# One block for three attention layers: a node queue across layers, three weight batches in the last, two rings of six

## The reference

```python
src_f = concatenate([src, loop]); dst_f = concatenate([dst, loop])      # every node has an edge to itself
def layer(h_in, p):
    h = h_in @ Wl
    a = (h @ asl)[src_f] + (h @ adl)[dst_f] + ea_f @ (Wel @ ael)
    a = where(a > 0, a, 0.2 * a)
    m = segment_max(a, dst_f); ea = exp(a - m[dst_f]); denom = segment_sum(ea, dst_f)
    out = segment_sum(h[src_f] * (ea / denom[dst_f])[:, None], dst_f) + bl
    return layernorm(out) * gl + bel
h, _ = scan(layer, x, (W, att_src, att_dst, W_e, att_edge, bias, ln_gamma, ln_beta))
x = layernorm(x + h)
```

## Time and profile before

| | |
|---|---|
| three timed runs | 4970.62, 4992.32, 4992.92 us (median 4992.32) |
| span of the profiled execution | 4946.1 us |
| time of the profiled execution as a whole | not recorded apart from its span |
| PE busy, mean granted clock | 3008.1 us (61%), 0.744 |
| DVE busy | 2621.4 us (53%) |
| ACT busy | 2248.3 us (45%) |
| POOL busy | 1924.2 us (39%) |
| HBM | 152 GB/s over the span |

### The profile page before, as it was taken

One profiled execution on the slowest core, in us unless ns is written; L12 is line 12 of the kernel. 1 busy time (PEld: TensorE's weight loads), 2 busy tenths in 40 slices (PEclk: granted clock), 3 DMA queues, 4 the chain that ended last, 5 costly groups with the idle time before them and its releaser, 6 DMA issues. The chain is left out here.

```text
span 4946.1 us, 67111 instructions
## 1 busy us (share of the span) xinstructions
PE 3008.1 (61%) x18033; PEld 2422.5 (49%) x18033; DVE 2621.4 (53%) x8048; ACT 2248.3 (45%) x5931; POOL 1924.2 (39%) x1994
## 2 busy tenths in 40 slices
PE   1183019997887786885663059981089930387864
PEld 1062007775443454443662049970089930377764
DVE  2083008998443665895662017760047730399875
ACT  0082008886111344674552027760057730387765
POOL 6605760000554554563665720007600047200366
PEclk7596559998777788997776569875589865698555
DMA  3293016664554343454663237652257642376542
GB/s 116 69 334 112 12 38 213 223 223 174 147 156 122 94 115 111 134 171 136 193 199 114 63 112 226 201 171 63 61 178 219 206 133 59 112 242 224 160 129 88
DMA packets 419336, 723.48 MB, mean 146 GB/s; under 512 B 76431, under 2 KB 137908, under 8 KB 418606
## 3 DMA queue, kind: packets, MB, share of 16 engines
q1 hardware_dynamic: 350990, 610.53, 37.7%
q0 software_dynamic: 63040, 107.35, 8.8%
q10 hardware_dynamic: 5024, 2.30, 0.2%
HBM read 428.65 MB, written 321.10 MB: 152 GB/s over the span
## 5 line engine op out<-in xcount | busy, mean ns | idle before, releaser
L663 POOL DMA_INDIRECT msgs<-t_gat,row_i x591 | 564.5, 955 | 1097.5 <-POOLq L161 913.7
L2193 ACT ACTIVATE t_nnt<-t_p_nt,cxt 128x512 f32<-128x512 f32 x294 | 200.5, 682 | 767.1 <-remote 250.6
L1718 PE MATMUL t_p_q<-mean_col,t_nsq 128*128 128x1 f32 x2352 | 336.7, 264 | 265.0 <-issue 242.3
L1718 PEld LDWEIGHTS t_p_q<-mean_col,t_nsq 128*128 128x128 f32 x2352 | 347.8, 227 | 273.0 <-issue 272.9
L679 POOL DMA_INDIRECT dg_g_ring<-t_xw,src_i x197 | 190.2, 965 | 653.9 <-DVE slot_id L1182 580.2
L2073 PE MATMUL t_p_nt<-ident,t_nh 128*128 128x128 f32 x1176 | 220.5, 320 | 306.8 <-issue 175.5
L1987 POOL DMA_INDIRECT out_rows<-t_x,own_i x197 | 201.4, 1022 | 487.1 <-ACT t_x L2243 433.0
L1711 PE MATMUL t_p_nh<-wx,t_nnt 128*128 128x132 f32 x1568 | 268.1, 323 | 175.3 <-issue 132.0
L2073 PEld LDWEIGHTS t_p_nt<-ident,t_nh 128*128 128x128 f32 x1176 | 161.0, 165 | 325.5 <-issue 229.9
L1711 PEld LDWEIGHTS t_p_nh<-wx,t_nnt 128*128 128x128 f32 x1568 | 231.3, 224 | 176.4 <-issue 175.8
L1732 DVE TENSOR_TENSOR t_nhn<-t_p_nh,t_ninv 128x264 f32<-128x264 f32 x392 | 151.4, 428 | 260.0 <-remote 143.2
(11 more groups left out here) (402 smaller groups left out, 8599.3 us busy)
## 6 DMA issues: line engine op xcount, KB each, us to landing
t_nh<-t_gat SPq DMA_DIRECT2D x294, 264.0 KB
t_gat<-t_nhn SPq DMA_DIRECT2D x196, 264.0 KB
t_x<-de_x SPq DMA_DIRECT2D x196, 256.0 KB
t_ah<-t_gat SPq DMA_DIRECT2D x150, 264.0 KB
t_x<-t_x SPq DMA_DIRECT2D x148, 256.0 KB
t_gat<-t_ahn SPq DMA_DIRECT2D x100, 264.0 KB
t_gat<-de_h SPq DMA_DIRECT2D x98, 264.0 KB
t_xw<-in_x_map SPq DMA_DIRECT2D x28, 903.0 KB
```

Source lines behind the costliest of these rows:

```text
L663: self.nc.gpsimd.indirect_dma_start(out=self.msgs[:, c, 0:width], out_offset=None, in_=table, in_offset=bass.IndirectOffsetOnAxis(ap=idx[: ...
L1718: last = self.nc.tensor.matmul(p_q[:, j:j + 1], sq[:, j * D:(j + 1) * D], self.mean_col[:], start=True, stop=True)
L2193: nc.scalar.activation(nnt[:, g % 2], p_nt[:], ACT.Identity, bias=bias).then_inc(act_nt, 1)
```

## The change

The three calls become one, `phase_gats`, with one block and one plan of 342 ticks for all three layers.

- The 294 node groups stand in one queue. It doesn't stop at the end of a layer: ticks 102 to 113 take the first groups of layer 1 beside the last slot groups of layer 0, and ticks 198 to 227 the first 30 of layer 2 beside the end of layer 1. The node part of a table depends on no slot, so only the gathers wait for the slot groups of the layer before: POOL waits for their stores (`rows_stored`) in place of the barrier.
- Layer 2 has three weight batches. Its pieces stand in ticks 257 to 264, 277 to 285 and 298 to 306. Slot groups 0 to 4 enter in ticks 265 to 269, the others from 292 on (`HELD` keeps them back), and the queue of nodes ends at tick 299. Of the ticks from 300 on 42 hold slot work alone.
- The ring `x` of ten is split: `xn` with six buffers for nodes, and `held`, six laid over the buffers of `nhn` and `ahn`, for slots. The rings `nh` and `ah` shrink from four buffers to three, `tt` from three to two.
- In the last stage the constant is added first (`slot_beta`, `node_beta`), and DVE scales one of a slot group's four tiles (`slot_scale`), where ACT scaled all four.

```diff
-XR = 10
+NR = 3
+XR = 6
-LAST_BATCHES = ((0, ROWP),)
-PLAN = BATCHES, (96, 190, 290), 2.6, 2.6
-LAST_PLAN = LAST_BATCHES, (280,), 3.4, 5.0
+READY = 96, 190, 290
+NODE_TIME = 2.6, 2.6, 3.4
+SUM_TIME = 2.6, 2.6, 5.0
+HELD = 240
...
+    for layer in range(L):
+        last = layer == L - 1
...
+            elif not own and pieces and at - begun >= READY[pieces[0][1]]:
+                w = pieces.pop(0)
+            held = last and a >= XR - 1 and at - begun < HELD
+            i = None
+            if a < end and (a < open_to or open_to == AG) and not held:
+                i, a = (layer, a), a + 1
+            m = None
+            if n < NODES + 6:
+                m, n = n, n + 1
+            plan.append((m, i, w))
...
             def _(pool):
-                for b, (r0, r1) in enumerate(batches):
-                    self.resident_gather(self.row_i, self.th[layer], XW, got[b], range(2 * r0, 2 * r1))
+                for layer in range(L):
+                    if layer > 0:
+                        rows_stored(pool, nout, layer * DG)
+                        rows_stored(pool, aout, layer * AG)
+                    for b, (r0, r1) in enumerate(BATCHES):
+                        self.resident_gather(self.row_i, self.th[layer], XW, got[b], range(2 * r0, 2 * r1))
...
+                for g in range(AG):
+                    pool.wait_ge(xa_act, g + 1)
+                    pool.wait_ge(xa_dve, g + 1)
...
+                        if g >= XR:
+                            sp.wait_ge(xput[g % XR], 16 * G4 * (g // XR))
+                        sp.dma_start(held[:, g % XR], self.slots(self.x3, 0, g)).then_inc(xarra[g % XR], 16)
...
+                def slot_result(k):
+                    act.wait_ge(xa_inv, k + 1)
+                    for j in range(G4 - 1):
+                        r = nc.scalar.activation(held[:, k % XR, j, :], held[:, k % XR, j, :], ACT.Copy, scale=iva[:, k % 3, j:j + 1])
+                    r.then_inc(xa_act, 1)
...
 def resnorm_gnn(nc, args, out):
-        for layer in range(3):
-            net.phase_gat(layer)
+        net.phase_gats()
```

More of the change, by code:

```diff
@@ L45 @@
 EVERY = 5
-XR = 10
+NR = 3
+XR = 6
+L = 3
+NODES = L * DG
 BATCHES = ((0, 32), (32, 64), (64, ROWP))
-LAST_BATCHES = ((0, ROWP),)
-PLAN = BATCHES, (96, 190, 290), 2.6, 2.6
-LAST_PLAN = LAST_BATCHES, (280,), 3.4, 5.0
[L53 to L71, removed]
+READY = 96, 190, 290
@@ L1930, in phase_gat @@
[L1930 to L1938, removed]
+            got = [sem(f"got{b}") for b in range(len(BATCHES))]
@@ L1957, in phase_gat @@
[L1957 to L1972, removed]
+                if a is not None and 0 <= a[1] - 3 < AG:
+                    roots["a", a[0] * AG + a[1] - 3] = len(roots) + 1
+            batch_of = lambda g: [b for b, (r0, r1) in enumerate(BATCHES) if 2 * r0 <= g * G4 < 2 * r1][0]
@@ L2046, in _ @@
+                for n, a, w in plan:
                     if n is not None:
@@ L2220, in sums @@
-                    if 0 <= i - 4 < AG and not last_layer:
-                        g = i - 4
-                        act.wait_ge(dve_ahn, g + 1)
-                        nc.scalar.activation(self.att_s[:, g * G4:(g + 1) * G4, :], ahn[:, g % 3, :, D:D + 3], ACT.Copy).then_inc(act_att, 1)
-                def weights(b, part):
-                    rows = slice(*batches[b])
+                        s = layer * AG + i - 2
+                        act.wait_ge(dve_as, s + 1)
+                        wait(act, pe_ah, s - 1)
@@ new lines, in slot_beta, with slot_row @@
+                def slot_beta(k):
+                    dve.wait_ge(xarra[k % XR], 16 * (k // XR + 1))
+                    nc.vector.tensor_tensor(held[:, k % XR], held[:, k % XR], self.each(self.bet[:]), ALU.add).then_inc(xa_bet, 1)
+                def slot_row(k, s):
+                    dve.wait_ge(xa_bet, k + 1)
+                    for j in range(G4):
+                        y = nc.vector.scalar_tensor_tensor(out=held[:, k % XR, j, :], in0=p_ah[:, k % 2, j * D:(j + 1) * D],
+                                                           scalar=ainv[:, s % 2, j:j + 1], in1=held[:, k % XR, j, :],
+                                                           op0=ALU.mult, op1=ALU.add)
+                    y.then_inc(xa_y, 1)
```

582 lines of the change are left out of this document (327 added, 255 removed).

## The result

The changed kernel took 4993.63 us (median of 20 runs, 4965.91 to 5014.46), the kernel before on the same chip 4967.69 us (20 runs, 4936.09 to 5010.7). The ratio is 1.0048, with a 95% interval of 1.003 to 1.0065: slower by half a per cent, at the edge of what I had called no change. The forecast was 5001 us, with +9 us for the change itself; the medians give +26. That 5001 lies only 7 us above 4993.63 is in part luck: the median that I started from, 4992.32, is 25 us above that of the 20 runs, and the change cost 17 us more than forecast.

What follows compares the result with a forecast made beforehand. PE bounds node groups in layers 0 and 1 and pairs, DVE slot groups and layer 2's node groups; gathers nearly dead, no engine full in the scatter. Terms sum to +9 us, giving 5001 us, range 4930 to 5070.

Steps and rivals of the forecast that it cites:

- step 6: Between the layers: two block ends go, -4 us (low -8, high 0).
- step 7: Last stage: DVE scales one tile of each slot group, 50 times, +6 us (0 to +12).
- step 8: Buffer rings: smaller rings, six held buffers and first slot loads no longer issued ahead, +2 us (0 to +40).
- step 4: Layer 2: two more weight batches, priced from the one of before, +38 us (+14 to +60).
- step 1: End of layer 0: 12 ticks of slot work become pairs with node groups, +15 us.
- step 2: End of layer 1, ticks 206 to 227: 22 mixed ticks of 6.7 us, +64 us (+60 to +113).
- step 3: Thirty node groups leave layer 2, -98 us; eight replace cheaper groups in layer 1, +9; together -89 us.
- step 5: Gathers of layers 1 and 2: more node groups use the 20 us before the stall, -23 us (-23 to 0).
- rival A: Scatter: constant, sum and scale no longer queue behind PE's late result; -48 us, to a total of 4953 us; chance 0.27.
- B: Ticks 206 to 227: PE's clock falls to 1.2 GHz, ticks take 8.9 us; +48 us, total 5055 us; chance 0.15.
- C: Scatter: SP waits for the ring of six, DVE behind it; +42 us, total 5043 us; chance 0.16 together with D.
- D: Layer ends: the stalled gathers keep the node queue from running ahead; +42 us; chance 0.16 together with C.

Runs made afterwards that it cites:

- second chip: Chip with the stall, where both kernels and variants of the change were run; kernel before 4934.5 us, changed kernel 4946.75 us, ratio 1.0031.
- first pair: First profiles of the kernel before and the unaltered changed kernel, compared layer by layer; the kernels' medians there were 4967.69 and 4993.63 us.
- third chip: Chip without the stall, where the unaltered change and variants of it were measured; kernel before 3437.27 us, changed kernel 3410.57 us, ratio 0.9927.

## Why the prediction came out, step by step

**The sum came right by luck.** On the second chip the change can be built up in three steps, from the medians, with intervals that don't meet from one kernel to the next:

| | measured | forecast |
|---|---|---|
| one block, rings, order of the last stage (steps 6 to 8) | +20 | +4 |
| three batches in layer 2 (step 4) | -38 | +38 |
| the pull (steps 1, 2, 3 and 5) | +30 | -33 |
| together | +12 | +9 |

The two largest parts have the wrong sign, by 76 and 63 us, and the errors cancel. The order matters: the pull and the batches both live on the node groups of layer 2, so with one batch the pull may cost less or nothing. That kernel was not run on a chip with the stall; on chips without it, it was as fast as the changed kernel.

**Steps 1 and 2 were right.** The mixed ticks took 6.8 and 6.9 us against 6.7, with PE at 0.73 to 0.74 of its clock, and layer 1 is longer by 75 us in the first pair of profiles (predicted 58, or 71 if the saving of step 5 is left out of it). Removing the pull (all but three groups of it) makes layer 1 shorter by 73 us, as much as step 2's 64 and the 9 that step 3 has there, and layer 0 by 18, against 15 of step 1. (The nearest rows that step 2 names have PE busy 80 and 81%, not 77 to 81; nothing hangs on it.)

**Step 3 was mis-sized.** It took each node group that leaves layer 2 at 3.28 us, 98 in all, the price of a group that stands alone. Removing the pull alone brings back 65 us. With three batches many of these groups would stand beside slot groups during the scatter, and there one costs 8.8 - 6.7 = 2.1 us. So its rule, that pairing saves only where one side is bound by PE, is refuted by its own stage: it also saves where DVE waits for something else. The first pair's -67 in layer 2 looks like the predicted -62 only because step 4 was wrong the other way.

**Step 4 had the wrong price, and without the pull the wrong sign.** +38 us stood there, for two more batches at what one had cost. Without the pull they were worth -38 us in the medians, 22 of them seen in layer 2. With the pull, on the chip without the stall, they cost 3 us in the medians and 11 in the spans, where one interval holds the other's ratio. That they cost nothing with the pull on a chip with the stall is argued, from layer 2's -67 and -84 us. I had read from the plan that only five slot groups go early; what counts is that early weights let slot groups, and their scatters, run beside node groups. This went unseen because I priced the batches and the pull apart: the pull has taken those node groups away by then.

**Step 5 failed.** I let the gathers use 20 us before the stall for 9 more node groups, -23 us. What came lies near its other end, 0: counted by ACT's first instruction for a group, 7, 6 and 6 node groups passed in the gathers of the three layers, against 6, 6 and 6; counted by DVE's first, 6, 7 and 6 against 5, 5 and 5. In layer 1 PE's results were late from 3 us after the first gather on, while in layer 0 of the kernel before ACT took them at once for more than 10 us (its transposes of 2645.50 end at 2646.59, and ACT goes on at 2646.63). So the stall doesn't follow the time since the first gather; what it follows is open. It isn't set off by the first products for the weights (`att_s`), which PE starts only at 3367.69.

**Steps 6, 7 and 8.** From DVE's last result to the gather it is 3.0 us after, 4.1 before, so -1 us for each end and not -2. Of the +2 and +6 us of steps 8 and 7 the scatter shows a sum: the tick rose by 0.45 us in the first pair and by 0.2 on the second chip, 19 and 8 us in 42 ticks, and on the second chip, with one batch, DVE's own work accounts for all of it. L2368 takes 0.31 to 0.33 us where 0.25 were predicted. The cover that step 8 named, a tick of 6.41 us against four scatters and a landing, was not enough, for SP waited 19.6 us for scatters; but the wait had no price of its own there. It may have taken what the earlier constant and sum would else have given (rival A's gain); a ring of seven or more was not tried. Where the rest of the +20 us lies (the three layers of these two profiles differ by +9) is open.

**The rivals.** A (a quicker scatter) did not happen with the stall: 6.9 and 6.7 us a tick, not 5.3 (only where the stall is absent did it come near, 5.6, and no profile of the kernel before was taken there). B did not: 0.73 to 0.74 of the clock and 6.9 us, not 8.9. C's waits came, its price did not. D did not: layer 2's first gather came 75 us later behind layer 1's than before, with some thirty of its node groups done. From the last gather to the end it is 628 us, within the 620 to 645 that were to show the forecast right: this sign could not tell the right argument from two errors that cancel.

## What to carry to other kernels

Moving work from one stage to another gains only where the target stage has idle time on the engine that the moved work needs, and what the source stage loses counts too: here the groups would have filled idle time in the scatter and were moved to where DVE was full. Price edits that feed on the same work together, not one by one, and check a forecast by its parts: here the total was right to 3 us with two parts wrong by over 60. A wait in a queue is no cost by itself: SP's for the scatters was longest where the scatter was quickest. Where a profile has a stretch in which all engines are nearly idle, measure on a second chip: this change is slower by 0.3 to 0.5% on chips with that stretch and faster by 0.7% on one without.

## What the hardware showed that I had not expected

The same program took 4934.5 us on one chip and 3437.27 us on another, 1.44 times, and each chip kept to its time (27 and 12 runs, within 0.6% and 0.7% from end to end). Of the 1545 us between the two spans of the changed kernel (4953.7 and 3408.8), 812 lie in the attention layers, which take 695, 754 and 865 us with the stall and 446, 485 and 572 without, and 733 ahead of them.

In the stall PE's results reach the engines that wait for them late, and nothing else that I looked at does. In the second chip's profile of the changed kernel, PE's timeline in the gathers of layer 1:

```profile
3343.09 0.63 PE L2083 MATMUL t_p_nt<-ident,t_nh 128*128 128x128 f32 x4 [1.09 <-issue]
3346.39 1.84 PE L1738 MATMUL t_p_q<-mean_col,t_nsq 128*128 128x1 f32 x8 [2.67 <-issue]
3352.53 2.10 PE L1731 MATMUL t_p_nh<-wx,t_nnt 128*128 128x132 f32 x8 [4.31 <-issue]
...
3367.76 1.09 PE L2083 MATMUL t_p_nt<-ident,t_nh 128*128 128x128 f32 x4 [7.15 <-issue]
3389.15 1.84 PE L1738 MATMUL t_p_q<-mean_col,t_nsq 128*128 128x1 f32 x8 [20.31 <-issue]
```

and the engines that take the results, first ACT, then DVE:

```profile
3366.35 0.69 ACT L2246 ACTIVATE t_nnt<-t_p_nt,cxt 128x512 f32<-128x512 f32 x1 [20.11 <-issue]
3366.93 0.68 ACT L2247 ACTIVATE t_nsq<-t_p_nt,cxt 128x512 f32<-128x512 f32 x1
3388.74 0.26 ACT L2252 ACTIVATE t_nsd<-t_p_q,eps 128x4 f32<-128x4 f32 x1 [21.13 <-remote]
```

```profile
3389.04 0.18 DVE L2390 RECIPROCAL t_ninv<-t_nsd 128x4 f32<-128x4 f32 x1 [28.81 <-issue]
3411.14 0.77 DVE L1752 TENSOR_TENSOR t_hn<-t_p_nh,t_ninv 128x264 f32<-128x264 f32 x2 [21.93 <-remote]
```

Each result of PE is taken before PE's next product of the same kind begins, so it is that of the earlier one. PE's transposes end at 3343.72, and ACT starts on them at 3366.35, 22.6 us later; the mean squares end at 3348.23, and ACT takes the root at 3388.74, 40.5 us later; the products with the weights end at 3354.63, and DVE scales them at 3411.14, 56.5 us later. ACT was free for the root only from 3367.61 and DVE for the scaling from 3389.22, so of these two delays 21.1 and 21.9 us are certainly waits for PE. The three come 22.4 us apart.

The other way there is no delay. ACT's squares end at 3367.61 and free `p_nt`, and PE's next transposes start at 3367.76; ACT's root ends at 3389.00 and frees `p_q`, and PE's next mean squares start at 3389.15. DVE follows ACT's root after 0.04 us. So PE's idle time before these products, which the profile puts down to "issue", is a wait for a buffer whose reader has itself waited for PE. Without the stall the results go over at once, on the third chip with as many gathers beside them: transposes that end at 2403.38, and ACT at 2403.42.

```profile
2402.78 0.60 PE L2083 MATMUL t_p_nt<-ident,t_nh 128*128 128x128 f32 x4
```

```profile
2403.42 0.69 ACT L2246 ACTIVATE t_nnt<-t_p_nt,cxt 128x512 f32<-128x512 f32 x1 [0.81 <-PE t_p_nt L2083]
```

They also do on the second chip, where POOL issues nothing: at the end of its layer 0 transposes end at 3331.31 (3330.71 + 0.60) and ACT starts at 3331.34. From 3200 to 3320, just before, the DMA engines are 68% busy with 206 GB/s, in the gathers from 3340 to 3580 27% with 65. So the amount of DMA traffic alone doesn't make it. In the scatter, where POOL issues indirect transfers again, the results are late again, by some 3 us.

What the profile can't tell is whether PE's products themselves end late (the ends in its rows are modelled) or the word of their end. That it needs POOL's indirect transfers fits all stretches that I looked at on chips with the stall, but whether their issuing, their landings or something else of the chip is the cause stays open: the five runs made for it fell on chips without the stall.
